# Logits products over 128 columns, rows gathered into their own records, and a new order of work in a fused FFN, RNN and FFN kernel

## The reference

```
x = x + 0.5 * ffn(layernorm(x))
x = x + rnn(layernorm(x))
x = x + 0.5 * ffn(layernorm(x))
```

## Time and profile before

| what | value |
|---|---|
| median of three runs | 580.89 us |
| profiled execution, its own time | 578.79 us |
| its span, first to last instruction | 576.4 us |
| PE busy | 532.8 us, 92% |
| POOL busy (rests among it) | 450.0 us, 78% |
| DVE busy | 405.9 us, 70% |
| ACT busy | 315.4 us, 55% |
| mean granted TensorE clock | 0.950 of 2.4 GHz |
| first scan step, last scan step | 116.7 us, 495.7 us |

### The profile page before, as it was taken

One profiled execution on the slowest core, in us unless ns is written; L12 is line 12 of the kernel. 1 busy time (PEld: TensorE's weight loads), 2 busy tenths in 40 slices (PEclk: granted clock), 3 DMA queues, 4 the chain that ended last, 5 costly groups with the idle time before them and its releaser, 6 DMA issues.

```text
span 576.4 us, 15923 instructions
## 1 busy us (share of the span) xinstructions
PE 532.8 (92%) x4541; PEld 520.4 (90%) x4541; DVE 405.9 (70%) x1485; ACT 315.4 (55%) x1104; POOL 450.0 (78%) x562
## 2 busy tenths in 40 slices
PE   6849998899999999999999999999999999988991
PEld 6848997899999999999999999999999999877991
DVE  4799486778686798697569865777586467784650
ACT  2222363556666666566665666666656665544560
POOL 2497887559898887088997989978998938899982
PEclk8666599999999999999999999999999999999996
DMA  7974822222222232133323333322332301435410
GB/s 246 274 267 167 253 89 69 74 67 74 75 68 86 73 79 62 39 93 108 93 65 79 106 110 100 91 61 75 93 103 80 108 20 70 144 125 143 115 40 0
DMA packets 54147, 58.88 MB, mean 102 GB/s; under 512 B 8983, under 2 KB 42018, under 8 KB 54064
## 3 DMA queue, kind: packets, MB, share of 16 engines
q1 hardware_dynamic: 43776, 36.15, 21.4%
q0 software_dynamic: 9440, 21.06, 11.6%
q10 hardware_dynamic: 848, 0.66, 0.5%
HBM read 27.67 MB, written 30.62 MB: 101 GB/s over the span
## 4 chain that ended last, share of the span: by engine, by line
PE 71%; POOL 8%; DVE 8%; issue 5%; DMA 3%; SPq 1%; ACT 1%; POOLq 0%; ACTq 0%; DVEq 0%
PE yp L1705 23%; PE hp L1695 22%; PE z L1715 11%; PE mT L1601 4%; PE xTp L1684 4%; POOL idle L1166 3%; POOL xy_dram L1183 3%; PE lg L1645 3%; PE z L1665 2%; POOL out_dram L1203 2%; DMA hsT<-in_L_attn_x_dram 2%; ACT s_sb L1513 1%; PE hp L1720 1%; DVE pay L1252 1%; DVE r_sb L1375 1%
## 5 line engine op out<-in xcount | busy, mean ns | idle before, releaser
L1705 PE MATMUL yp<-projT,s_sb 128*128 x1248 | 204.0, 292 | 8.5 <-ACT s_sb L1513 8.2
L1695 PE MATMUL hp<-xT_sb,w_sb 128*128 128x128 f32 x1248 | 200.7, 289 | 0.3 <-ACT w_sb L1504 0.2
L1705 PEld LDWEIGHTS yp<-projT,s_sb 128*128 128x128 f32 x1248 | 164.1, 193 | 10.9 <-issue 10.8
L1695 PEld LDWEIGHTS hp<-xT_sb,w_sb 128*128 128x128 f32 x1248 | 166.0, 196 | 1.7 <-issue 0.5
L1484 ACT ACTIVATE hsT<-z 128x16 f32<-128x16 f32 x512 | 93.7, 183 | 134.1 <-PE z L1715 124.4
L1715 PE MATMUL z<-hsT,wT 128*128 128x16 f32 x1024 | 156.7, 229 | 0.1
L1715 PEld LDWEIGHTS z<-hsT,wT 128*128 128x128 f32 x1024 | 153.7, 190 | 3.2 <-ACT hsT L1484 0.3
L1513 ACT ACTIVATE s_sb<-r_sb 128x256 f32<-128x256 f32 (+1 forms) x260 | 114.2, 452 | 63.0 <-DVE r_sb L1375 31.6
L1375 DVE TENSOR_SCALAR r_sb<-hp 128x512 f32<-128x512 f32 x156 | 106.9, 685 | 56.9 <-PE hp L1695 54.8
L1166 POOL MEMSET idle<- 128x600 f32 x229 | 141.8, 619 | 0.2
L1504 ACT ACTIVATE w_sb<-fc_sb 128x256 f32 (+1 forms) x259 | 112.8, 455 | 4.6 <-issue 2.2
(11 more groups left out here) (133 smaller groups left out, 502.4 us busy)
## 6 DMA issues: line engine op xcount, KB each, us to landing
xs_sb<-xs_dram SPq DMA_DIRECT2D x71, 129.0 KB, 2.2
xy_dram<-zeros SPq DMA_DIRECT2D x11, 512.0 KB, 5.1
xs_sb<-xy_dram SPq DMA_DIRECT2D x85, 64.0 KB, 1.9
xy_dram<-y_sb SPq DMA_DIRECT2D x85, 64.0 KB, 1.6
hsT<-in_L_attn_x_dram SPq DMA_DIRECT2D x14, 256.0 KB
hsT<-n_L_ffn_expert_proj_dram SPq DMA_DIRECT2D x2, 1024.0 KB, 16.3
fc_sb<-in_L_ffn_expert_fc_dram SPq DMA_DIRECT2D x1, 2048.0 KB
out_dram<-y_sb,xs_sb POOLq DMA_INDIRECT x71, 2.6
```

The costliest lines, as they stand in the source:

```text
L1695: mm = pe.matmul(hp[:, g % 2, h * P:(h + 1) * P], w_sb[:, g % 2, h * P:(h + 1) * P], xT_sb[:, g % 2, :], start=True, stop=True)
L1705: mm = pe.matmul(yp[:, 0:D], s_sb[:, g % 2, h, :], projT[:, bass.ds(offsets[g] + h * D, D)], start=(h == 0), stop=(h == HC - 1))
```

## The change

The logits product moves 128 columns. Columns 8 to 127 of what moves are zeros that POOL writes once at the start; the zeros' results land in the PSUM bank of the logits behind the 8 wanted columns and are written over by the next block's product (the product is cut at the bank's end). The rows of the first FFN are gathered into the XN columns of their own records, so that `back` and the wait for unit u - 3 go. RING is 16 for 12.

The plan changes with it. SECOND cuts the second FFN's units into ten routes for seven and MIDDLE cuts the units before the scan into fourteen groups for thirteen. `AHEAD` puts the input rows of units 6 and 7 ahead of the load of the projections. `plan` costs a logits product at 128 columns, its guess of the clock has another rule, `fill` counts from PE's last work (`worked`) and also applies while one tile is ordered, gathers are given to POOL's list as soon as the tile is stored, puts are held back when the last route is about to be placed (`keep`), and pieces of the last route may go ahead of the tile's work on DVE (`end`). The weights in PR are others.

```diff
-MIDDLE = [1, 1, 1, 1, 1, 1, 1, 1, 1, 2, 2, 2, 1]
-SECOND = [4, 3, 3, 2, 2, 1, 1]
+MIDDLE = [1, 1, 2, 1, 1, 1, 1, 1, 1, 1, 1, 2, 1, 1]
+SECOND = [4, 3, 1, 2, 1, 1, 1, 1, 1, 1]
-RING = 12
+RING = 16
-BACK = 3
-AHEAD = [2, 4, 7]
+AHEAD = [5, 7, 7]
...
+            if ("pick", second[-1]) in ev and second[-1] not in sorted_out:
+                soon = [p for p in pool_wait if p[1][0] != "put" or max(pool_free, p[0]) < ev["pick", second[-1]] + PR["keep"]]
+                start = max(pool_free, min([p[0] for p in soon], default=limit))
+                if start >= limit:
+                    return
...
-                n = int((need[0] - pe) / 0.25) if not order else 0
+                n = int((max(need[0], pe) - worked) / 0.25) if len(order) <= 1 else 0
...
-                hurry = isinstance(job[0], Middle) and (job[0].u0 * UNIT - t) * 0.66 < PR["crit"]
+                hurry = (job[0].u0 * UNIT - t) * 0.66 < PR["crit"] if isinstance(job[0], Middle) else job[0] and job[0].second and job[0].last and PR["end"] > 0
...
-                held += [(ev["free", g], r, u) for u in done]
+                pool_wait += [(ev["free", g], ("gather", r, u, j)) for u in done for j in range(UR)]
...
-        wT = sb("wT", [P, 2 * P + E])
+        wT = sb("wT", [P, 3 * P])
+            pool.memset(wT[:, 2 * P + E:], 0.0).then_inc(s_const, 1)
...
-                    if u >= BACK:
-                        pool.wait_ge(s_add, add_no[u - BACK])
-                    out=back[:, u % BACK, j, :], out_offset=None, in_=xy1_dram[r.index],
+                    out=pay[:, n, XN:XN + D], out_offset=None, in_=xy1_dram[r.index],
...
-                    j = 4 * i + q
-                    mm = pe.matmul(lg[:, j * E:(j + 1) * E], xrt[:, m % XRING, q * P:(q + 1) * P], rwT, start=True, stop=True)
+                    at = (4 * i + q) * E
+                    n = min(P, 512 - at)
+                    mm = pe.matmul(lg[:, at:at + n], xrt[:, m % XRING, q * P:(q + 1) * P], wT[:, 2 * P:2 * P + n], start=True, stop=True)
```

More of the change, by code:

```diff
@@ L213, in plan @@
     lg_owner, lg_last, lg_after, given, sorted_out = None, None, {}, set(), set()
-    turns_of, logits_of, est, held = [], [], {}, []
-    clock, begun, busy, moved = 1.0, 0.0, 0.0, 0.0
+    turns_of, logits_of, est = [], [], {}
+    clock, begun, moved, worked = 1.0, 0.0, 0.0, 5.0
     def ahead_of(r):
@@ L367, in matmuls @@
     def matmuls(n, columns, need):
-        nonlocal pe, clock, begun, busy, moved
+        nonlocal pe, clock, begun, moved, worked
         at = max(pe, need)
@@ L427, in split @@
                 if p[0] == "logits":
-                    return passes(place, 4, 8, (("turn", p[1], p[2]), lg_after[p[1].index]), p if half else None)
+                    return passes(place, 4, 128, (("turn", p[1], p[2]), lg_after[p[1].index]), p if half else None)
                 return passes(place, 4, 128, (("turn2", p[1]), ("h", UNIT * (p[1] - 1) - 1) if p[1] >= 2 else None), p if half else None)
@@ L859, in build @@
         xnT = sb("xnT", [P, ZRING, 512])
-        back = sb("back", [P, BACK, UR, D])
         fc_sb = sb("fc_sb", [P, E * HD])
@@ L1731, in split @@
                     inputs(piece[1], half)
-            pe.wait_ge(s_const, 10)
+            pe.wait_ge(s_const, 11)
             warm_up(EARLY)
```

38 lines of the change are left out of this document (19 added, 19 removed).

## The result

The changed kernel takes **588.6 us** (583.7 to 592.4 over four executions) against 580.6 (577.3 to 581.5) for the kernel before on the same chip: a ratio of **1.0137, interval 1.0092 to 1.0181**. The forecast was 570.4 with a range to 579.5. The profiled execution took 585.9 us (span 584.1, granted clock 0.975) where that of before took 578.8 (576.4 and 0.950). So the clock is better, as forecast, and the time is worse.

What follows compares the result with a forecast made beforehand. PE was taken as the bound from 118 to 489 us, with gains only before and behind. -3.0 - 5.4 - 3.0 - 1.5 + 2.4 = -10.5 took the span from 576.4 to 565.9, the median to 570.4 us; range 563 to 579.5.

Steps and rivals of the forecast that it cites:

- The clock: Front, 12 to 18 and 56 to 72 us: with 128-column logits PE's clock stays at 2.4 GHz (1.00).
- Rivals 2 and 3: Zeros don't raise the clock, 578.8 us, chance 0.08; 256 wide passes cost 0.025 us more each, 576.8 us, chance 0.03.
- First scatter, -3.0: Front: full clock and an earlier `pick` send the first scatter out sooner, -3.0 us, bounds -4.7 and 0.
- so the first tile comes sooner by as much: Front: all sixteen scatters follow at 1.75 us each, so the first scatter's gain reaches the first tile whole.
- Tiles 0 to 4, -5.4: From 60 to 72 us: 63 passes at full clock take 7.2 us for 12.0; with smaller gains -5.4, bounds -7.1 and 0.
- near 108: Sign that the forecast is right: the first scan step comes near 108 us.
- Gathers and rings, 0: Scan and loads: POOL's wait before gathers and SP's for puts go, but PE hardly waited for them; 0 us.
- Finer routes, -3.0: Before the scan's end: units 12 and 13 as own routes let tiles replace fillers at 489 us; -3.0, bounds -5.3 and 0.
- The chain after the last step, -1.5: Last step to the last part's first load, 27.3 us: `place` starts 2.1 us sooner; -1.5, bounds -5.0 and +1.
- What the new plan adds, +2.4: Three more routes' work on DVE, PE and POOL: up to three stalls of 1.45 us, 4.4 us; +2.4 taken, new weights included.
- Rival 4: Scan: unit 4's gathers go ahead of the third route's last scatters, POOL stands, PE loses 10 us; 585 us, chance 0.13.

Runs made afterwards that it cites:

- e2: The changed kernel with the logits product back at 8 columns; ratio 1.011 to the kernel before.
- e1: The kernel before with the 128-column logits alone, its order kept; 577.9 us, ratio 0.9977.
- h1: e1 with five pieces of DVE's work in the front moved, for an earlier first scatter; 574.5 us, ratio 0.9964.
- g1: The changed kernel in its own order, with identity products that nothing reads ahead of twelve stalled PE instructions; 583.5 us, ratio 1.0108.
- i1: h1 with two more normalisations moved earlier, so that the second route's scatters start sooner; 572.0 us, ratio 0.9911.
- i2: The changed kernel with normalisations and statistics in its front moved to start both routes' scatters earlier; 580.4 us beside 576.3 for the kernel before, no interval.
- e3: The kernel before with gathers into their own records and no wait for an addition, narrow logits; 580.5 us, ratio 1.0011.
- e4: The changed kernel's code, weights and middles with the kernel before's seven second routes instead of ten; 579.2 us, ratio 1.0048.
- e7: The changed kernel with the weight `end` at 0, the last route's pieces behind the tile's work on DVE again; 583.7 us, ratio 1.0122.
- f3: The changed kernel with six pieces of DVE's work moved later, off the stalls; 586.9 us, ratio 1.0193.
- e5: The changed kernel's code with the routes, cuts and weights of the plan before; 593.0 us, ratio 1.0236.
- g2: e1 with identity products in nine of its PE stalls; ratio 0.998.

## Why the prediction was wrong

1. **The clock**: right. It is at 1.00 from 12 to 18 us and from 56 to 72, wide passes take 0.112 us, and zeros keep it up; with narrow logits in the same order it was at 0.50 from 14.6 to 18.0 and from 52.1 to 69.2 (e2). Rivals 2 and 3 are out.
2. **First scatter, -3.0**: the size was right at its own place (4.1 us sooner), and needs the order as well as the clock. With wide logits in the old order the logits are done by 13.9 us, `pick` still stands behind the normalisation at 15.97, and the scatter is 0.9 us sooner (e1); with `pick` ahead of it, as the forecast had it, it is 3.8 to 4.1 (h1, changed kernel). That the width is what frees the clock there is not shown: in e2 the clock was at 1.00 up to 14.6 us with narrow logits, and the scatter left at 20.31. The step "so the first tile comes sooner by as much" was wrong. The new order spends it on the 5.60 us wait: the first load is issued at 56.4 us for 54.2, and the 5.4 us of the first output come behind that load, where the clock was down before.
3. **Tiles 0 to 4, -5.4**: the outputs of tiles 0 to 4 take 9.1 us for 10.5, the eleventh comes 3.4 us sooner. The step that failed is the one that let both terms run to the first scan step, "near 108". I looked for what PE would find to do and not at what else stands ahead of the first gather. POOL's list does: 16 scatters and a root, to 91.8 us in the changed kernel. In fourteen other traces too the gather leaves directly behind that root, between 90.8 and 93.2 us (all but e2, g1, i1 and i2), and i1 moved it by starting the list sooner. The new plan also sets three more tiles ahead of the first step, 6.4 us, which the scan is spared. Forecast about -9, measured +3.1: of the 18 us between the forecast span of 565.9 and the 584.1 that came, 12 lie in the front, and 5 to 6 of them if these tiles are left out.
4. **Gathers and rings, 0**: right for the gathers (e3). The ring of 16 was not tested alone.
5. **Finer routes, -3.0**: the fillers before the last steps are gone as forecast, but e4 shows the three routes, with the order that the plan makes for them, to cost 5 us. The sign was wrong in this plan.
6. **The chain after the last step, -1.5**: it is 26.0 us for 27.3 (from 502.71 to 528.74), and PE pays 4.82 us of stall and 6.8 us of half clock for it. The stretch is 1.0 us longer, which one trace doesn't tell from none; e7 shows that undoing it wins nothing that can be measured.
7. **What the new plan adds, +2.4**: the term that was mis-sized most, and the step that failed in the scan. I priced three stalls of 1.45 us at their length, and took the new order for nearly free. The scan has 8.0 us more idle time, and up to 5.1 us are lost at half clock behind it, 13.1 us. In the trace of before no stall in the scan was over 0.83 us, so nothing there showed the price of one. The Trainium skill (TensorE: Matmul & The Clock Gate, Part 1) has the clock go back to half when the engine has been idle. That is the direction seen here; but the falls came behind stalls around which PE had been busy for most of the time (2.94 of 4.70 us from 161.0), which that wording does not lead one to expect. With the 1.8 us that one fall costs (16 passes missing from 315.9 on) the bound of three stalls would have been 9.8 us and not 4.4. That is still below 13.1, because the number of stalls was wrong as well as their price.
8. **Rival 4**: its side came true and its mechanism didn't. The third route's scatters run from 132 to 188, the gathers of unit 4 from 191.5.

What stays open: which order of DVE's pieces would take the 10 us of idle time out of the new scan. Fewer routes leave most of the stalls (e4), and moving six pieces moves them on (f3). A lighter DVE was not tried. Which of the plan's new rules makes the worse order is open too: e5 holds them all together with the ring of 16, and no run takes one of them, or the ring, alone.

## What to carry to other kernels

A head start is worth what is left of it at the next engine that has a list of its own: follow it through each in-order queue to the first instruction that was idle before, and start that list sooner first (two moved pieces here, 4.0 us). In a stretch in which TensorE is the bound, price a new stall at its length plus the half clock that may follow it, and look for the longest stall that the kernel has now. Half clock in a stretch where the engine waits anyway costs little: e1 loses 13.6 us less to it than the kernel before and starts its scan 3.4 us sooner, and 10.2 us less than e3, and starts 0.2 us sooner. Compare two traces of one order before a difference of 3 us between two orders is given a cause.

## What the runs showed of the hardware

- Of 25 stalls of 1.4 us and more in the scans, 17 had 3.4 to 17.1 us at 1.2 GHz behind or from within them: all eight over 2.1 us, nine of the seventeen shorter ones. The executions of one kernel differ in granted clock, the changed kernel's from 0.961 to 0.976, and spread over 8.7 us; g2, with no fall from 45 us to the last tiles, spreads over 1.1.
- Products of the identity in the stall keep the clock at 2.4 GHz (116 passes for 63 in 13.4 us).
- Small int32 conversions on DVE take 0.17 us as a rule, and 0.59 to 0.73 us at some places (L1348 and L1349 at 312 us in the changed kernel); `place` and the first piece of `list` of the second FFN's second route, 2.8 us by the plan's own guess, took 4.3 there. What slows them was not measured by itself.
